# Expert tiles move out of the third and fourth attention round of a one-core decoder layer

## The chip, the core and the metric

The kernel runs on one core of one Trainium2 chip, in one launch. The metric is the device time of an execution in microseconds. Three executions of the kernel before took 701.37, 704.38 and 706.86 us; the median, 704.38 us, is its time.

## What is computed

4096 tokens (64 sequences of 64) of width 128 go through three blocks, each with a residual and a layer norm. Cut to what matters:

```python
def layer(x, ctx):
    x = layernorm(x + state_space_scan(x))                      # 16 states per channel, sequential in time
    x = layernorm(x + gated_linear_attention(q=x, k=ctx, v=ctx)) # 4 heads, exp-gated, causal over 64 tokens
    return layernorm(x + ffn(x))

def ffn(x):                                   # 8 experts, the top 2 for each token, hidden width 512
    probs = softmax(x @ gate_w)
    weight, index = top_k(probs, 2); weight = weight / weight.sum(-1)
    for i in range(8):
        wi = where(index == i, weight, 0).sum(-1)
        h = silu(x @ w1[i]) * (x @ w3[i])
        out += (h @ w2[i]) * wi
    return out
```

## The kernel before

Five instruction lists are written out by hand, one per engine (PE, ACT, DVE, POOL, and SP, which only issues transfers), and tied by semaphores. Each list runs in order. So a list's order is the schedule: an instruction that waits holds back all that stands behind it on its engine.

The tokens are eight chunks of 512 (`NCH = 8`). The first part, up to about 284 us, is the scan, eight steps for each chunk. Then come the attention rounds, c = 0 to 8. Round c on DVE (`attend_round`) normalizes the attention output of chunk c, makes the weights of chunk c + 1 from the scores, and routes chunk c - 1: logits, the two best experts, ranks by PE, and the places of each token's row in a buffer in DRAM sorted by expert. POOL sends these rows there with eight indirect transfers (`send_rows`, L736) at the head of the next round. PE's list for a round has four groups of scores (L979), the transposes of chunk c - 1 (L1008), its logits (L1018), two groups of products with the values (L997), and the rank products (L1028 to L1035).

The experts' work is cut into tiles. The first 25 (`WIDE`) are double tiles of 256 rows of one expert; 21 single tiles of 128 rows are left for the end. A double tile is two units. A unit is two products with `w1` (L1063 into `py` or `pB`), two with `w3`, a Silu on ACT (L1361), and a product on DVE (L1789). The first unit of a tile also carries the product with `w2` of the tile before it (L1076, `down`), scaled on ACT and scattered by POOL (L745). Each tile needs its rows (`load_x`, six buffers) and 768 KB of weights (`load_w`, four buffers). Weights of tile i wait for `down` of tile i - 4.

Which expert and which rows a tile holds is found on the chip. `wide_table`, at the end of a DVE round, turns the counts so far into places for the next tiles, in 17 small operations that each wait for the one before, and three that update the account; `tab_done` is raised. `batch_of(i)` tells which table tile i belongs to. `load_x` waits for this table and for POOL to have sent the rows of all chunks that the table counts.

Where the tiles stand is told by `first_tiles(c)`, spread over the first half of round c's lists, and `second_tiles(c)`, over the second half. Before, these were tile 0 in round 3, tiles 1 and 2 in round 4, and four tiles in each of the rounds 5 to 8; the tiles from 19 on (`LAST_TILES`) lie behind the rounds, six double ones and the 21 single ones. SP loads the second tiles of a round at the head of its round, ahead of the keys (`load_heads`, L493), maxima (`load_m`, L485) and values (`load_v`, L501) of the rounds to come, and the first tiles of the next round behind them. The first input transpose of tiles 0 and 1 (`FRESH`) is placed by hand in rounds 3 and 4; that of any other tile comes with the unit before it. ACT switches its function table between Silu and the logarithm and exponential within a round (`log_exp_table`).

## Time and profile before

| what | us |
|---|---|
| median of three executions | 704.38 |
| the profiled execution | 706.54 |
| its span, first to last instruction | 704.9 |
| TensorE busy | 544.6 (77%) |
| VectorE busy | 430.6 (61%) |
| ScalarE busy | 329.5 (47%) |
| GpSimd (POOL) busy | 369.7 (52%) |
| mean granted TensorE clock | 0.863 of full |

The profile page gives the busy time of each engine, the span in 40 slices, the chain of work that ended last and the costliest groups of instructions. Busy shares are means over stages with different limits, so a change within the attention rounds is read from the rounds: from the timeline of an engine, where each row is a group of instructions with its start, its length, and in brackets how long the engine was idle before it and what ended that, and from windows, one row for each stretch of time: its length, the busy us of PE, PE's weight loads, DVE, ACT and POOL (with their instructions), the granted clock of PE, the DMA engines' busy share and GB/s. The windows shown below are rounds 1, 3, 4, 5, 6 and 7.

### The profile page before, as it was taken

What the parts mean: (1) busy time and instruction counts of PE and PEld (TensorE: products, weight loads), DVE (VectorE), ACT (ScalarE), POOL (GpSimd) and SP (SyncE); (2) the same over time, 40 slices, a digit from 0 to 9 for tenths busy, and PEclk for the clock granted to TensorE, in tenths of its full rate; (3) what the DMA queues carried; (4) which work ended last, traced back from release to release, by engine and by line L of the source; (5) the groups of instructions that cost most, each with busy time, mean ns of one, the idle gap of its engine ahead of it and who ended that gap; (6) DMA issues with size and microseconds to landing.
All of it is one profiled execution on the core that took longest, in us unless ns stands there. A gap on an engine that the chain in (4) does not pass through costs nothing.

```text
span 704.9 us, 10813 instructions
## 1 busy us (share of the span) xinstructions
PE 544.6 (77%) x3387; PEld 386.7 (55%) x3387; DVE 430.6 (61%) x880; ACT 329.5 (47%) x732; POOL 369.7 (52%) x301
## 2 busy tenths in 40 slices
PE   2589999899889888686384889797878689989800
PEld 0234434445344447675263768686667568988800
DVE  1599999999999941676748376656352612211155
ACT  2475685876867553122132435444443323333327
POOL 1497979999789752216506163625253533322341
PEclk9999999999999995555555789998898899999955
DMA  4434535444454532732341735361616157788594
GB/s 148 148 101 148 175 122 166 146 170 167 137 179 146 191 74 52 133 62 62 77 113 42 193 120 158 136 232 36 203 63 216 59 177 243 241 292 270 170 244 117
DMA packets 83319, 104.51 MB, mean 148 GB/s; under 512 B 40784, under 2 KB 64592, under 8 KB 83136
## 3 DMA queue, kind: packets, MB, share of 16 engines
q1 hardware_dynamic: 74576, 90.99, 42.4%
q0 software_dynamic: 4320, 8.92, 3.7%
q10 hardware_dynamic: 4368, 3.93, 2.0%
q8 instruction: 27, 0.44, 0.3%
q14 instruction: 28, 0.23, 0.1%
HBM read 91.48 MB, written 12.34 MB: 147 GB/s over the span
## 4 chain that ended last, share of the span: by engine, by line
PE 25%; issue 24%; POOL 20%; DVE 10%; DMA 9%; ACT 3%; SPq 2%; another core or an unknown queue 1%; POOLq 0%; ACTq 0%; DVEq 0%
POOL hc L640 12%; PE pB L1063 7%; PE pq L1076 4%; DMA wslot<-in_expert_w 4%; PE py L818 4%; PE py L1063 2%; POOL y_dram L745 2%; PE pC L997 1%; ACT x_all L1457 1%; DMA y_dram<-dx,xin 1%; PE pa L979 1%; POOL xg_dram L736 1%; DMA x_all<-y_dram 1%; POOL bcs L604 1%
## 5 line engine op out<-in xcount | busy, mean ns | idle before, releaser
L640 POOL TENSOR_TENSOR hc<-h,Crep 128x1024 f32<-128x1024 f32 x64 | 149.7, 2356 | 14.6 <-DVE h L1507 13.2
L745 POOL DMA_INDIRECT y_dram<-dx,xin x71 | 68.9, 971 | 153.9 <-ACT dx L1378 144.8
L1063 PE MATMUL pB<-Crep,wslot 128*128 128x256 f32 (+1 forms) x556 | 118.9, 360 | 21.9 <-DMA wslot<-in_expert_w 10.7
L818 PE MATMUL py<-hc,ident 128*128 128x512 f32 x256 | 120.7, 598 | 8.1 <-POOL hc L640 8.1
L1063 PEld LDWEIGHTS pB<-Crep,wslot 128*128 128x128 f32 x556 | 90.8, 204 | 38.7 <-DMA wslot<-in_expert_w 14.0
L1498 DVE TENSOR_TENSOR u<-dx,pC 128x1024 f32<-128x1024 f32 x64 | 77.3, 1207 | 17.4 <-PE pC L807 17.3
L818 PEld LDWEIGHTS py<-hc,ident 128*128 128x128 f32 x256 | 46.8, 189 | 53.9 <-issue 37.4
L1789 DVE TENSOR_TENSOR Crep<-u,pB 128x512 f32<-128x512 f32 x35 | 24.0, 686 | 85.5 <-PE pB L1063 42.2
L1507 DVE TENSOR_TENSOR_SCAN h<-pB,u 128x1024 f32<-128x1024 f32 x32 | 73.1, 2285 | 1.0 <-ACT pB L1196 0.6
L1507 DVE TENSOR_TENSOR_SCAN h<-pa,u 128x1024 f32<-128x1024 f32 x32 | 73.1, 2284 | 0.0
L1789 DVE TENSOR_TENSOR u<-u,pB 128x512 f32<-128x512 f32 x36 | 24.8, 688 | 78.9 <-PE pB L1063 46.0
L736 POOL DMA_INDIRECT xg_dram<-x2r,idx x32 | 33.4, 1043 | 41.1 <-DVE idx L1733 32.6
L1378 ACT ACTIVATE dx<-pq,xin 128x128 f32<-128x128 f32 x71 | 23.4, 366 | 66.5 <-PE pq L1076 62.5
L807 PE MATMUL pC<-bcs,sel 96*128 96x512 bf16 x128 | 39.0, 386 | 15.6 <-DVE u L1498 10.0
L1196 ACT ACTIVATE pa<-delta,Aneg 128x512 f32<-128x512 f32 x64 | 41.5, 681 | 20.2 <-DVE h L1507 18.5
L1196 ACT ACTIVATE pB<-delta,Aneg 128x512 f32<-128x512 f32 x64 | 41.5, 679 | 12.4 <-DVE h L1507 12.4
L979 PE MATMUL pa<-x1T_all,dx 32*64 32x64 f32 x512 | 31.7, 289 | 19.6 <-DVE h L1587 8.9
L1063 PE MATMUL py<-Crep,wslot 128*128 128x256 f32 (+1 forms) x180 | 42.3, 370 | 2.6 <-DMA wslot<-in_expert_w 2.5
L1361 ACT ACTIVATE u<-pB 128x512 f32<-128x512 f32 x36 | 21.5, 598 | 47.0 <-PE pB L1063 27.8
L736 POOL DMA_INDIRECT xg_dram<-x2r_last,idx_last x32 | 32.2, 1006 | 19.1 <-DVE idx_last L1733 10.6
L979 PEld LDWEIGHTS pa<-x1T_all,dx 32*64 32x64 f32 x512 | 26.3, 192 | 26.2 <-issue 17.8
L1076 PE MATMUL pq<-wslot,u 128*128 128x128 f32 x288 | 37.8, 283 | 1.3 <-issue 1.3
(225 smaller groups left out, 952.0 us busy)
## 6 DMA issues: line engine op xcount, KB each, us to landing
wslot<-in_expert_w SPq DMA_DIRECT2D x46, 768.0 KB
Crep<-c_dram SPq DMA_DIRECT2D x64, 512.0 KB, 3.8
h<-m_dram SPq DMA_DIRECT2D x16, 256.0 KB
xin<-xg_dram SPq DMA_DIRECT2D x25, 130.0 KB
cT_st<-in_ctx_T SPq DMA_DIRECT2D x8, 256.0 KB, 4.1
dx<-in_ctx_T SPq DMA_DIRECT2D x8, 256.0 KB, 4.0
delta<-in_ctx_tok SPq DMA_DIRECT2D x32, 64.0 KB
hc<-y_dram SPq DMA_DIRECT2D x8, 256.0 KB, 8.5
```

Of the source, the lines that this page charges most:

```text
L640: nc.gpsimd.tensor_tensor(hc[:, K % 4], h[:, K % 3], Crep[:, K % 4].rearrange("p a t -> p (a t)"), ALU.mult).then_inc(hc_done, 1)
L736: nc.gpsimd.indirect_dma_start(out=xg_dram, out_offset=bass.IndirectOffsetOnAxis(ap=places[:, m:m + 1], axis=0), in_=rows[:, k, b], in_off ...
L745: nc.gpsimd.indirect_dma_start(out=y2_dram, out_offset=bass.IndirectOffsetOnAxis(ap=xin[:, i % NX, a, D:D + 1].bitcast(i32), axis=0), in_= ...
L807: last = nc.tensor.matmul(pC[:, i], sel[:, 2 * k + i], bcs[:, c % 2], start=True, stop=True)
L818: last = nc.tensor.matmul(py[:], ident[:], hc[:, K % 4, i * CH:(i + 1) * CH], start=False, stop=(K % STEPS == STEPS - 1 and i == 1))
L979: last = nc.tensor.matmul(pa[S * j:S * j + S, 0, s0:s0 + S], cTc[rows, t0:t0 + S], x1T_all[rows, c * CH + t0:c * CH + t0 + S], start=True, ...
L1063: last = nc.tensor.matmul(bank[:, o * a * P:(o + 1) * a * P], wslot[:, i % NW, stage * F + f * P:stage * F + (f + 1) * P], xgT[i % 2][:, 0 ...
L1076: last = nc.tensor.matmul(pq[:, PAIR + t * P:PAIR + (t + 1) * P], hs[i % 2][:, at:at + P], wslot[:, i % NW, 2 * F + f * D:2 * F + (f + 1) ...
L1196: last = nc.scalar.activation(bank[:, i], delta[:, c % 2], ACT.Exp, scale=Aneg[:, n:n + 1])
L1498: nc.vector.tensor_tensor(u[:, K % 3].rearrange("p (a t) -> p a t", a=2), dx[:, c % 2].unsqueeze(1).to_broadcast([P, 2, CH]), pC[:], ALU.m ...
L1507: nc.vector.tensor_tensor_scan(h[:, K % 3], bank[:].rearrange("p a t -> p (a t)"), u[:, K % 3], 0.0, ALU.mult, ALU.add).then_inc(h_done, 1)
L1789: nc.vector.tensor_tensor(hs[i % 2][:, k * F:(k + 1) * F], sil[:, n % 2], pB[:, 1], ALU.mult).then_inc(mul_done, 1)
```

## The change

Tile 0 no longer stands in round 3 nor tiles 1 and 2 in round 4. Round 5 has five tiles: 0 and 1 in its first half, 2 to 4 in its second. Rounds 6 to 8 have four each (5 to 16), and the tiles from 17 on lie behind the rounds, eight double ones. The first table is made at the end of round 3 in place of round 2 and holds five tiles in place of one, so there is one table less and each tile's number of tables to wait for is one less. SP loads tiles 0 and 1 at the end of its round 3. Only tile 0's transpose is placed by hand, in round 4. ACT's table switches leave rounds 3 and 4.

```diff
--- before.py
+++ after.py
@@ -385,7 +385,7 @@
 
             if i >= WIDE:
                 return NCH
-            return 2 + (i - 1) // TB if i else 1
+            return 2 + max(i - 1, 0) // TB
 
         def first_unit(i):
 
@@ -401,13 +401,15 @@
 
         def first_tiles(c):
 
-            return range(TB * (c - 5) + 3, TB * (c - 5) + 5) if c >= 5 else range(0)
+            if c == 5:
+                return range(0, 2)
+            return range(TB * (c - 5) + 1, TB * (c - 5) + 3) if c >= 6 else range(0)
 
         def second_tiles(c):
 
-            if c == 3:
-                return range(0, 1)
-            return range(TB * (c - 4) + 1, TB * (c - 4) + 3) if c >= 4 else range(0)
+            if c == 5:
+                return range(2, TB + 1)
+            return range(TB * (c - 5) + 3, TB * (c - 4) + 1) if c >= 6 else range(0)
 
         def units(tiles):
 
@@ -504,7 +506,7 @@
             def load_x(i):
                 b = batch_of(i)
                 a = halves(i)
-                sp.wait_ge(tab_done, b)
+                sp.wait_ge(tab_done, b - 1)
                 top_row = E * REG + (SPARE - 1) * P if a == 1 else E * REG - PAIR
                 row = sp.value_load(rowt[0:1, i:i + 1], min_val=0, max_val=top_row)
                 sent = min(b, NCH - 1)
@@ -549,7 +551,9 @@
                 if c == 2:
                     store_m(1)
                     load_m(c + 3)
-                if 4 <= c < NCH:
+                if c == 3:
+                    load_tiles(first_tiles(5))
+                if 5 <= c < NCH:
                     load_tiles(first_tiles(c + 1))
             before, behind = range(LAST_TILES.start, WIDE - 2), range(WIDE - 2, WIDE)
             load_tiles(before)
@@ -1078,7 +1082,7 @@
                                                 start=(f == 0), stop=(f == FB - 1))
                 last.then_inc(dn_done, 1)
 
-            FRESH = (0, 1)
+            FRESH = (0,)
 
             def expert_units(numbers):
                 for n in numbers:
@@ -1127,8 +1131,8 @@
                 if front:
                     scores(c + 1, 3)
                     weighted_values(c + 1, 0)
-                if c in (3, 4):
-                    turn_x(c - 3)
+                if c == 4:
+                    turn_x(0)
                 expert_units(second[0:1])
                 if front:
                     weighted_values(c + 1, 1)
@@ -1379,7 +1383,7 @@
                                                 scale=xin[:, i % NX, a, D + 1:D + 2])
                 last.then_inc(y_cp, 1)
 
-            FRESH = (0, 1)
+            FRESH = (0,)
 
             def expert_units(numbers):
                 for n in numbers:
@@ -1419,7 +1423,7 @@
                 if mid:
                     square_heads(c)
                 expert_units(first[1:2])
-                if mid and c >= 4:
+                if mid and c >= 5:
                     log_exp_table()
                 if front:
                     weight_decay(c + 1)
@@ -1430,10 +1434,10 @@
                     copy_rows(c - 1)
                 if c == 3:
                     floor_gates(1)
-                if c in (3, 4):
-                    copy_xT(c - 3)
+                if c == 4:
+                    copy_xT(0)
                 expert_units(second[0:2])
-                if c >= 3:
+                if c >= 5:
                     log_exp_table()
                 if back:
                     share_exp(c - 1)
@@ -1771,11 +1775,11 @@
 
             def wide_table(c):
 
-                n = 1 if c == 1 else TB
-                if c == 1:
+                n = TB + 1 if c == 2 else TB
+                if c == 2:
                     dve.wait_ge(const_step, CONSTS)
                 dve.wait_ge(ranks_read, c + 1)
-                table(region, ALU.is_ge, PAIR, TB * (c - 2) + 1 if c > 1 else 0, n)
+                table(region, ALU.is_ge, PAIR, TB * (c - 2) + 1 if c > 2 else 0, n)
                 tlink(nc.vector.tensor_scalar(cum[:], cum[:], float(PAIR * n), None, ALU.min))
                 tlink(nc.vector.tensor_tensor(given[:, 0:E], given[:, 0:E], cum[:], ALU.add))
                 tlink(nc.vector.tensor_tensor(given[:, 1:E], given[:, 1:E], cum[:, 0:E - 1], ALU.subtract))
@@ -1855,7 +1859,7 @@
                 if c == 3:
                     log_norm(1)
                 attend_round(c)
-                if c >= 2:
+                if c >= 3:
                     wide_table(c - 1)
                 if c == 0:
                     keep_gates(NCH - 1)
```

Three places of the lists, before and after. The lines of the changed kernel are two to four higher.

VectorE at the end of round 2, before. `idx_last` are the places of chunk 1's rows; what follows is the table, up to the running maximum `mrow` and the next round's first operation `norm`.

```order
L1733 CAST idx_last<-posf 128x8
L1750 TENSOR_TENSOR cnt<-carry,region 128x8
L1751 TENSOR_TENSOR ysq<-cnt,kstep 128x8x16
L1753 TENSOR_REDUCE ntl<-ysq 128x8
...
L1766 CAST eoff<-tsum 128x1
L1768 CAST rowt<-tsum 128x1
L1779 TENSOR_SCALAR cum<-cum 128x8
L1780 TENSOR_TENSOR given<-given,cum 128x8
L1781 TENSOR_TENSOR given<-given,cum 128x7
L1537 SCALAR_TENSOR_TENSOR mrow<-fence,pq 128x128
L1542 TENSOR_TENSOR nlog<-cs_sb,pq 128x48
L1596 TENSOR_TENSOR norm<-pC,floor_ 128x16
```

The same place now:

```order
L1737 CAST idx_last<-posf 128x8
L1541 SCALAR_TENSOR_TENSOR mrow<-fence,pq 128x128
L1546 TENSOR_TENSOR nlog<-cs_sb,pq 128x48
L1600 TENSOR_TENSOR norm<-pC,floor_ 128x16
L1579 TENSOR_TENSOR u<-u,g_sb 128x1024
```

The table is gone from this place; the first one stands at the end of round 3.

TensorE in the second half of round 3, before: `pa` are scores, `pC<-delta,h` the products with the values, `xin` the tile's rows, `wslot` its weights, `mask` the ranks.

```order
L979 MATMUL pa<-x1T_all,dx 64x64 x16
L997 MATMUL pC<-delta,h 64x33 x16
L1046 MATMUL pq<-ident,xin 128x128 x2
L1063 MATMUL pB<-Crep,wslot 128x256 x4
L997 MATMUL pC<-delta,h 64x33 x16
L1063 MATMUL py<-Crep,wslot 128x256 x2
L1063 MATMUL pB<-Crep,wslot 128x256 x2
L1028 MATMUL pC<-mask,tri_s 128x32
```

The same stretch now:

```order
L983 MATMUL pa<-x1T_all,dx 64x64 x16
L1001 MATMUL pC<-delta,h 64x33 x32
L1032 MATMUL pC<-mask,tri_s 128x32
```

The tile's transpose and its eight products have left round 3. In round 4 only tile 0's transpose stands between the two groups of products with the values.

VectorE at the end of round 5, before (`u<-u,pB` or `Crep<-u,pB` is a unit's product, `pos` the first operation on the ranks):

```order
L1712 TENSOR_TENSOR x2r<-share 128x4
L1789 TENSOR_TENSOR u<-u,pB 128x512
L1650 TENSOR_SCALAR xT<-plog,mv,rstd 128x128 x4
L1789 TENSOR_TENSOR u<-u,pB 128x512
L1718 TENSOR_TENSOR pos<-pC,carry 128x32
L1722 TENSOR_TENSOR carry<-carry,pC 128x8
```

The same place now:

```order
L1716 TENSOR_TENSOR x2r<-share 128x4
L1793 TENSOR_TENSOR Crep<-u,pB 128x512
L1654 TENSOR_SCALAR xT<-plog,mv,rstd 128x128 x4
L1793 TENSOR_TENSOR Crep<-u,pB 128x512
L1793 TENSOR_TENSOR u<-u,pB 128x512 x2
L1722 TENSOR_TENSOR pos<-pC,carry 128x32
L1726 TENSOR_TENSOR carry<-carry,pC 128x8
```

Two more unit products, those of the fifth tile, stand ahead of the ranks.

## Rows read from the trace of the kernel before

**Rows 1.** Windows by round: length, busy PE, PEld, DVE, ACT, POOL, PEclk, DMA.

```profile
303.00:319.30 16.30, 11.75 (x150) 10.36 (x149) 15.03 (x57) 4.33 (x10) 2.35 (x1) 0.50 0.34 62
...
343.90:376.50 32.60, 22.04 (x202) 17.37 (x200) 17.97 (x76) 9.30 (x17) 10.00 (x9) 0.55 0.40 93
376.50:412.50 36.00, 26.98 (x242) 23.06 (x242) 21.29 (x77) 15.13 (x28) 14.88 (x14) 0.74 0.56 155
412.50:449.40 36.90, 33.05 (x284) 28.21 (x284) 23.71 (x80) 17.92 (x34) 18.51 (x18) 0.91 0.46 144
449.40:486.10 36.70, 30.35 (x252) 25.59 (x252) 21.87 (x81) 17.84 (x34) 16.18 (x17) 0.95 0.39 130
486.10:522.50 36.40, 30.84 (x167) 26.14 (x168) 19.17 (x73) 16.89 (x33) 15.34 (x17) 0.86 0.38 129
```

**Rows 2.** Timeline of VectorE: where rounds 1, 3, 4 and 5 begin and end.

```profile
303.04 0.17 DVE L1596 TENSOR_TENSOR norm<-pC,floor_ 128x16 f32<-128x16 f32 x1
...
319.02 0.17 DVE L1733 CAST idx<-posf 128x8 int32<-128x8 f32 x1
...
338.61 0.17 DVE L1733 CAST idx_last<-posf 128x8 int32<-128x8 f32 x1
...
342.75 0.42 DVE L1537 TENSOR_TENSOR_SCAN mrow<-fence,pq 128x128 f32<-128x128 f32 x1
...
343.86 0.17 DVE L1596 TENSOR_TENSOR norm<-pC,floor_ 128x16 f32<-128x16 f32 x1
...
376.45 0.17 DVE L1596 TENSOR_TENSOR norm<-pC,floor_ 128x16 f32<-128x16 f32 x1
...
408.19 0.17 DVE L1733 CAST idx_last<-posf 128x8 int32<-128x8 f32 x1
...
412.49 0.17 DVE L1596 TENSOR_TENSOR norm<-pC,floor_ 128x16 f32<-128x16 f32 x1
```

**Rows 3.** Timeline of VectorE in the tail: first unit products of two tiles.

```profile
575.87 0.69 DVE L1789 TENSOR_TENSOR Crep<-u,pB 128x512 f32<-128x512 f32 x1 [3.83 <-PE pB L1063]
...
587.54 0.69 DVE L1789 TENSOR_TENSOR Crep<-u,pB 128x512 f32<-128x512 f32 x1 [1.28 <-PE pB L1063]
```

**Rows 4.** Timelines of POOL and SP in round 4: first send, loads of tile and keys.

```profile
373.12 0.98 POOL L736 DMA_INDIRECT xg_dram<-x2r,idx  x1 [20.46 <-DVE idx L1733]
...
385.44 0.40 SPq L517 DMA_DIRECT2D xin<-xg_dram  x1
...
389.35 0.43 SPq L493 DMA_DIRECT2D dx<-in_ctx_T  x1
```

**Rows 5.** Timeline of PE: waits for rows and weights, rounds 4, 6 to 8, tail.

```profile
391.17 3.78 PE L1063 MATMUL pB<-Crep,wslot 128*128 128x256 f32 x8 [1.91 <-DMA wslot<-in_expert_w]
...
466.61 1.99 PE L1063 MATMUL pB<-Crep,wslot 128*128 128x256 f32 x8 [0.59 <-DMA wslot<-in_expert_w]
...
499.42 0.44 PE L1046 MATMUL pq<-ident,xin 128*128 128x128 f32 x2 [0.91 <-DMA xin<-xg_dram]
...
503.11 2.65 PE L1063 MATMUL pB<-Crep,wslot 128*128 128x256 f32 x8 [2.39 <-DMA wslot<-in_expert_w]
...
539.22 1.99 PE L1063 MATMUL pB<-Crep,wslot 128*128 128x256 f32 x8 [2.00 <-DMA wslot<-in_expert_w]
...
573.78 1.99 PE L1063 MATMUL pB<-Crep,wslot 128*128 128x256 f32 x8 [2.52 <-DMA wslot<-in_expert_w]
```

**Rows 6.** Timeline of PE: the last two groups of scores, rounds 1 and 3.

```profile
309.64 2.29 PE L979 MATMUL pa<-x1T_all,dx 32*64 32x64 f32 x32 [2.00 <-DVE h L1587]
...
352.86 2.29 PE L979 MATMUL pa<-x1T_all,dx 32*64 32x64 f32 x32 [3.61 <-DVE h L1587]
```

**Rows 7.** Timeline of VectorE in round 3: the copy of the logits.

```profile
351.17 0.19 DVE L1667 COPY lgc<-pC 128x32 f32<-128x32 f32 x1 [3.26 <-remote]
```

**Rows 8.** Timeline of PE in round 5: the same four products, early and later.

```profile
416.88 2.05 PE L1063 MATMUL py<-Crep,wslot 128*128 128x256 f32 x4
...
425.83 1.13 PE L1063 MATMUL py<-Crep,wslot 128*128 128x256 f32 x4
```

## What the change is predicted to do

> **What bounds the kernel now.** I read the granted clock and span first, then the page's slices, then the busy times of each attention round (the windows [rows 1]), then the timeline of VectorE (DVE), whose in-order list marks where each round begins [rows 2], then PE, SP and POOL inside the rounds, and last the steady part of the tail. A round begins on DVE with `norm<-pC,floor_` (L1596). So round 1 begins at 303.04, round 3 at 343.86, round 4 at 376.45, round 5 at 412.49. The reader is to see two kinds of round. Round 1 has no expert tile and takes 16.3 us. Rounds 5 and 6 carry four double tiles each in 36.9 and 36.7 us, with PE busy for 33.05 and 30.35 us at a granted clock of 0.91 and 0.95 [rows 1]: they are near PE's bound. Rounds 3 and 4 carry one and two double tiles, yet take 32.6 and 36.0 us at a clock of 0.55 and 0.74 [rows 1]. So the first three tiles are the dearest of all: over a bare round with a table (16.3 + 4.3 us, the table's size is worked out below) they cost 68.6 - 41.2 = 27.4 us together, 9.1 each, where a double tile behind the rounds takes 5.84 us (rows of products 11.67 us apart over two tiles [rows 3]). The reason stands in the same rows: their matmuls run at the half clock, their two banks of products are waited for in DVE's order ahead of routing work, and in round 4 the tile's own rows and weights arrive late, because SP can load them only once POOL has sent the routed rows: POOL's first send is at 373.12, SP's load at 385.44, and PE's first product waits for the weights until 391.17 [rows 4, 5].
>
> **The change part by part.** All sums are made against the profiled execution: 706.54 us, of which the span is 704.9 and 1.6 lies around it. It is 2.2 us (0.3%) above the median of 704.38; I carry the difference over to the median.
>
> Round 2 loses its table (17 small DVE operations and three that update the account). idx_last is written at 338.61 and the next operation that stays, `mrow`, stands at 342.75 [rows 2]: 4.14 us. In order without the table the next operation follows in about 0.1 us. DVE is alone on the path here, since PE's transpose and round 3 both wait for `mrow`. So -4.0 us. The table of round 3 now makes five places in place of four; its instructions are the same number and one column longer, nothing to count.
>
> Round 3 without its tile: from its start to the two last score products is 352.86 - 343.86 = 9.0 us, which stays as it is [rows 2, 6]. From there a bare round goes on as round 1 does: 309.64 to the places at 319.02 is 9.4 us. Then the table, from places to the next round: 408.19 to 412.49, 4.3 us [rows 2, 6]. That is 22.7 us against 376.45 - 343.86 = 32.6. So -9.9 us. Those 9.0 us hold a wait of 3.26 us that the trace puts to "remote" [rows 7], at DVE's copy of the logits; I leave it in. If it goes, 3.3 us more are saved.
>
> Round 4 without its two tiles: 319.02 - 303.04 = 16.0 us for a bare round up to the places, and 4.3 for the table: 20.3 us against 412.49 - 376.45 = 36.0 [rows 2]. So -15.7 us. Up to here 29.6 us are saved, and round 5 begins near 383.
>
> Round 5 gets a fifth double tile. Its two units stand behind one another at the end of the round (the piece of order shows four products in a row, where two stood). Nothing of DVE's is between them, and DVE's ranks, places and table wait behind them. So they cost the steady rate of the tail: +5.8 us [rows 3]. Lower bound: nothing, if they fill idle time of PE, but PE is idle for only 3.9 of 36.9 us there. Upper bound: what a tile costs in round 4, (36.0 - 20.3)/2 = 7.9 us. I take 5.8.
>
> What the start of round 5 meets is new. The tiles 0 and 1 are loaded by SP behind round 3's loads, and must wait for POOL's sends: from the first send to the load it was 385.44 - 373.12 = 12.3 us [rows 4]. The places of round 3 come at about 358.2, so the sends begin at about 359.1 and the load goes out at about 371.4. Queued behind it on SP are tile 0's weights, tile 1, and then the keys of round 5's scores (`dx`), 3.9 us later (385.44 to 389.35 [rows 4]), at about 375.3. PE would ask for them at the end of round 4, some 14 us after its start at 362.5, so at about 376.5; with two weight tiles ahead of them on the same engines they may land at 380 or 381. PE then stands for up to 4 us, while DVE still has until 382.8 + 2.5 us of its own work. PE also turns tile 0 in round 4, between the two products with the values: it waits perhaps 1 us for the rows. I take +1.5 us, bounds 0 and 5.
>
> Round 5 starts at the half clock, as before: the same four products took 2.05 us at 416.88 and 1.13 us at 425.83 [rows 8]. The idle 3.9 us of PE lie at the start of the round, where the logits wait for DVE, then and now. What is new is that the two rounds in front are cold too. I add nothing for it in the sum and keep it as a rival.
>
> Rounds 6 to 8 and the tail keep their number of tiles per round, but every tile is now one to two tiles older when used: round 6 takes 5 to 8 where it took 7 to 10. Before, the third tile of each of these rounds is of the newest batch. It waits for POOL's sends through SP, and PE stands for the weights: 0.59 us in round 6, 0.91 and 2.39 in round 7, 2.00 in round 8, 2.52 in the tail [rows 5]. In the changed order the third tile of round 6 is of a batch whose table was made in round 4. Its load waits for nothing but a free place among four. So the 5.9 us of rounds 6 to 8 should go. Bounds: 0 (another wait takes their place) and 9 (round 7 also runs part of its time at the half clock, mean 0.86 [rows 1]). I take -5.
>
> The tail has eight double tiles in place of six: two at 5.84 = +11.7 us [rows 3]. But the newest tile (21) is now fifth in the tail where it was third, so the wait of 2.5 us goes too: +9.2 us. The 21 single tiles and all behind them are untouched.
>
> Sum: -4.0 - 9.9 - 15.7 + 5.8 + 1.5 - 5.0 + 9.2 = -18.1 us. On the profiled execution that is 688.4; on the median 686.3. What hid some of this was never idle DVE time: rounds 3 and 4 were long because their tiles stood inside DVE's list, so moving them out shortens the rounds at once, and what is late next is the bare round's own chain (DVE 15.03 us busy of 16.3 in round 1 [rows 1]).
>
> **Rivals.** A: less is gained. The waits of the late weights are replaced and not removed (+5), the 3.3 us stall of round 3 comes once more in round 4 as PE and DVE go through their lists faster (+3), and round 5's keys cost the whole 5 (+3.5 over mine) with part of these together: about 9 us, so 695. For it: stalls put to no visible cause stand in the bare stretches (3.26 us [rows 7]). Against it: round 1 has none.
>
> B: more is gained. The stall of round 3 goes (-3.3), the late loads give the full 9 (-4), the keys are hidden (-1.5): 8.8 more, about 677.5. For it: round 7 has no scores to make and still takes 36.4 us [rows 1], so its waits and its slow clock do set its length.
>
> C: slower. The clock. In rounds 3 and 4 PE now has only some 12 us of work in each 20, as in round 1 with its clock at 0.50 [rows 1]. If the gate stays at half through the whole of round 5, its products take 2.05/1.13 = 1.8 times as long. PE's work there is 33 us, of which about 3 are the price of the slow start, plus 5.8: 36 us at the full clock, 65 at half. With the 3.9 idle that is 69 us where I have 44, and 2 more at the start of round 6: +27, so about 713. It decides from where the half clock lasts over two thirds of round 5. Against it: in round 5 the clock was back within 9 us, between the products at 416.88 and 425.83 [rows 8], out of a round that began after an idle stretch as well. The Trainium skill (TensorE: Matmul & The Clock Gate, What's actually happening) says that the default state is throttled and activity releases it. By that rule the dense start of round 5 gives the clock back, and the row agrees; the two idle rounds ahead of it would cost nothing more.
>
> D: no change: round 5's five tiles and the tail's two take what they took where they were (9.1 us each): 27.4 us given back of 29.6, so about 702. Against it: the price of those three was the half clock, the late rows and the tables around them, none of which moves along.
>
> **How the numbers follow.** My case 0.66, with its own range 680 to 694; A 0.15; B 0.12; D 0.04; C 0.03. The predicted time is 686.3. The range reaches over A and most of B: 676 to 698. A measurement of this kernel can tell about 1% (7 us) from no change. Faster by over 1% means under 697.3: my case, B and most of A, 0.91. Within 1%: the rest of A and D, 0.06. Slower: C, 0.03.
>
> **What would show it.** In the changed profile: round 3 near 23 us and round 4 near 20 with no L1067 product in them; no DVE work between `idx_last` and `mrow` in round 2; round 5 at 43 to 46 us, with the half clock over before its second tile is through; no DMA wait of PE over 1 us in rounds 6 to 8 nor at the tail's fifth tile; round 7 at 33 us or less; 12 us more between the tail's first product and its first single tile, less 2.5. I am wrong if round 4 stays above 25 us, if round 5 goes over 50, or if PE's waits for weights come back in rounds 6 to 8.

## The result, and the profile after

The changed kernel takes 673.14 us (median of four, 670.91 to 674.23) where the kernel before took 702.91 beside it: a ratio of 0.9564 [0.9514, 0.9615]. I had forecast 686.3, with a range of 676 to 698. The direction was right; the gain is 29.8 us where I had 18.1, and the time falls below the range. Between the two profiled executions, spans 704.9 and 669.3, it is 35.6 us: the changed kernel's profiled execution was its fastest, and that of the kernel before, at 706.54 us, lies 3.6 above this median.

The changed kernel was measured in five batches of runs, and in two of them (one of these a single execution) it took 684 us, with stalls in its trace that the section on the hardware describes; I compare runs of one batch, or name it. The changed kernel was not run beside newest_wait, tile0_round3 and tiles01_round4; their traces show none of the stalls, so they are set against 673.14.

The windows of the changed kernel, one row a stage, with the columns of [rows 1]: rounds 2 to 8 (the last ends at the places), the table behind it, the eight double tiles of the tail, its single tiles.

```profile
319.30:337.80 18.50, 11.06 (x138) 9.76 (x140) 16.01 (x58) 4.32 (x10) 11.67 (x10) 0.50 0.25 61
337.80:360.00 22.20, 14.17 (x184) 12.38 (x182) 19.55 (x73) 5.13 (x12) 13.33 (x12) 0.50 0.56 103
360.00:381.30 21.30, 10.34 (x133) 9.28 (x133) 19.28 (x73) 4.11 (x10) 11.03 (x10) 0.50 0.53 146
381.30:421.90 40.60, 39.38 (x345) 33.17 (x344) 25.84 (x83) 22.13 (x42) 19.27 (x18) 0.97 0.65 189
421.90:458.30 36.40, 31.51 (x252) 27.07 (x252) 21.79 (x80) 17.90 (x34) 16.19 (x16) 0.91 0.41 130
458.30:490.00 31.70, 29.38 (x170) 24.73 (x170) 19.64 (x77) 16.76 (x33) 15.91 (x17) 0.89 0.47 151
490.00:511.10 21.10, 20.59 (x124) 16.72 (x122) 9.00 (x34) 11.45 (x23) 12.58 (x14) 1.00 0.60 205
511.10:520.00 8.90, 3.38 (x24) 2.75 (x22) 7.47 (x35) 1.55 (x5) 6.12 (x7) 0.82 0.49 158
520.00:567.50 47.50, 46.73 (x260) 38.50 (x261) 11.00 (x16) 15.24 (x37) 16.96 (x18) 0.93 0.53 169
567.50:630.20 62.70, 60.47 (x509) 58.34 (x508) 13.76 (x20) 22.64 (x60) 20.11 (x21) 1.00 0.80 269
```

Read it against [rows 1]: rounds 3 and 4 are bare (22.2 and 21.3 us for 32.6 and 36.0), round 5 is now the densest round (PE busy 39.4 of 40.6 us, clock 0.97), round 7 lost 5 us, and round 8 is all PE: 20.59 of 21.10 us at the full clock. That last row is the one I had not foreseen. The marks of DVE's list, which answer [rows 2]:

```profile
336.60 0.17 DVE L1737 CAST idx_last<-posf 128x8 int32<-128x8 f32 x1
336.68 0.41 DVE L1541 TENSOR_TENSOR_SCAN mrow<-fence,pq 128x128 f32<-128x128 f32 x1
337.78 0.17 DVE L1600 TENSOR_TENSOR norm<-pC,floor_ 128x16 f32<-128x16 f32 x1
...
360.01 0.17 DVE L1600 TENSOR_TENSOR norm<-pC,floor_ 128x16 f32<-128x16 f32 x1
...
381.25 0.17 DVE L1600 TENSOR_TENSOR norm<-pC,floor_ 128x16 f32<-128x16 f32 x1
```

`mrow` follows `idx_last` at once: the table has left round 2. The stages one by one, in us, from such marks; "second trace" is another execution of the kernel before (the first experiment).

| stage | forecast | before | second trace | after |
|---|---|---|---|---|
| round 2 | -4.0 | 24.5 | 22.6 | 18.5 |
| round 3 | -9.9 | 32.6 | 29.8 | 22.2 |
| round 4 | -15.7 | 36.0 | 36.2 | 21.2 |
| round 5 | +7.3 | 36.9 | 36.9 | 40.6 |
| round 6 | | 36.7 | 36.6 | 36.5 |
| round 7 | | 37.0 | 35.4 | 31.7 |
| round 8 to the places | -5.0 for 6 to 8 | 29.6 | 31.8 | 21.1 |
| places to the tail's first product | 0 | 9.0 | 8.9 | 8.9 |
| double tiles of the tail | +9.2 | 37.5 | 40.3 | 47.5 |
| single tiles | 0 | 66.4 | 66.2 | 62.7 |

### The profile page after: what moved, and what is told of

It is laid out like the page before. It is cut to its first block, busy times and chain, and to the rows that moved or that the text cites. A ratio compares the mean times of both kernels' runs of the same rounds, so it can differ in the third digit from the quotient of the medians.

```text
span 669.3 us, 10788 instructions
## 1 busy us (share of the span) xinstructions
PE 534.1 (80%) x3387; PEld 378.9 (57%) x3387; DVE 433.3 (65%) x862; ACT 321.8 (48%) x727; POOL 371.1 (55%) x301
## 4 chain that ended last, share of the span: by engine, by line
PE 32%; POOL 21%; issue 15%; DVE 13%; DMA 7%; ACT 4%; SPq 1%; POOLq 0%; ACTq 0%; DVEq 0%
POOL hc L644 13%; PE pB L1067 10%; PE pq L1080 5%; PE py L822 4%; PE py L1067 3%; POOL y_dram L749 2%; PE pa L983 2%; DMA dx<-in_ctx_T 2%; ACT x_all L1461 1%; PE pC L1001 1%; DMA y_dram<-dx,xin 1%; DMA x_all<-y_dram 1%; PE pq L1050 1%; POOL xg_dram L740 1%; DMA Crep<-c_dram 1%
## 5 line engine op out<-in xcount | busy, mean ns | idle before, releaser
L822 PE MATMUL py<-hc,ident 128*128 128x512 f32 x256 | 122.2, 605 | 7.9 <-POOL hc L644 7.9
L1067 PE MATMUL pB<-Crep,wslot 128*128 128x256 f32 (+1 forms) x556 | 113.4, 348 | 7.7 <-DVE Crep L1793 6.8
L1067 PEld LDWEIGHTS pB<-Crep,wslot 128*128 128x128 f32 x556 | 87.2, 198 | 23.3 <-DVE Crep L1793 10.4
L811 PE MATMUL pC<-bcs,sel 96*128 96x512 bf16 x128 | 39.0, 386 | 15.7 <-DVE u L1502 10.2
L1200 ACT ACTIVATE pa<-delta,Aneg 128x512 f32<-128x512 f32 x64 | 41.4, 678 | 20.3 <-DVE h L1511 18.4
L740 POOL DMA_INDIRECT xg_dram<-x2r_last,idx_last x32 | 32.6, 1019 | 23.6 <-DVE idx_last L1737 15.0
L1067 PE MATMUL py<-Crep,wslot 128*128 128x256 f32 (+1 forms) x180 | 39.4, 352 | 1.0 <-DMA wslot<-in_expert_w 1.0
L729 POOL TENSOR_TENSOR u<-maskT,h 128x1024 f32<-128x1024 f32 x8 | 18.8, 2352 | 35.6 <-ACT h L1329 20.6
```

What stands on the lines that cost most here:

```text
L740: nc.gpsimd.indirect_dma_start(out=xg_dram, out_offset=bass.IndirectOffsetOnAxis(ap=places[:, m:m + 1], axis=0), in_=rows[:, k, b], in_off ...
L811: last = nc.tensor.matmul(pC[:, i], sel[:, 2 * k + i], bcs[:, c % 2], start=True, stop=True)
L822: last = nc.tensor.matmul(py[:], ident[:], hc[:, K % 4, i * CH:(i + 1) * CH], start=False, stop=(K % STEPS == STEPS - 1 and i == 1))
L1067: last = nc.tensor.matmul(bank[:, o * a * P:(o + 1) * a * P], wslot[:, i % NW, stage * F + f * P:stage * F + (f + 1) * P], xgT[i % 2][:, 0 ...
L1200: last = nc.scalar.activation(bank[:, i], delta[:, c % 2], ACT.Exp, scale=Aneg[:, n:n + 1])
```

## Experiments

All are the changed kernel with one edit, unless said. The ratio is to the kernel before, run in the same batch.

**The kernel before, once more** (no edit; 704.65 us, one execution).

> The kernel before, once more, for a second trace. Theory 1 (the stalls that the first trace of it puts to no cause, 4.5 us in round 2, 3.3 us in round 3 and 4.7 us of DVE at the start of round 8, belong to the instruction lists): they stand again in the same places, within 1 us. Theory 2 (they belong to that one execution): at least two of the three are gone and the time is 3 to 6 us under the first profile's 706.5.

The stalls of rounds 2 and 3 that had no cause in the first trace are gone (22.6 and 29.8 us), but the time is only 1.9 us below the 706.54 of the first profile. In round 8 a wait stands plainly that the first trace had covered up. PE's timeline there:

```profile
529.23 0.69 PE L1046 MATMUL pq<-ident,xin 128*128 128x128 f32 x2 [6.34 <-DMA xin<-xg_dram]
...
532.38 3.78 PE L1063 MATMUL pB<-Crep,wslot 128*128 128x256 f32 x8 [0.76 <-DMA wslot<-in_expert_w]
```

PE waits 6.34 us for the rows of the newest tile, then 0.76 for its weights, and the eight products behind it run at the half clock, 3.78 us in place of 1.99 [rows 5]. In the first trace the same place showed a wait of 2.00 us. So what the older tiles take away in round 8 is about 10 us and not 2. A third trace (before_ref2) has the same rounds 2 and 3 and the same wait, 6.35 us for the rows.

**The wait put back** (newest_wait). SP waits for the sends of the newest places before it loads the second half of the tiles of rounds 6 to 8, so that the third tile of each of these rounds waits for what it waited for in the kernel before:

```diff
             for c in range(-1, NCH + 1):
+                if c >= 6:
+                    sp.wait_ge(rows_sent[c % 2], 128 * ((c - 2) // 2 + 1))
                 load_tiles(second_tiles(c))
```

> The changed kernel, in which SP, before it loads the second tiles of rounds 6, 7 and 8, waits until POOL has sent the rows of that round's newest chunk, as the kernel before had to. Theory 1 (the late weights are what shortened rounds 7 and 8 by 5.3 and 7 us): PE waits 0.5 to 3 us for weights again in each, its clock falls there, and the time rises by 6 to 12 us, to 679 to 685. Rival (those rounds were long by stalls of other kinds): PE's waits come back but the time rises by under 3 us.

Measured: 695.17 us, ratio 0.9879 [0.9834, 0.9924]. PE's timeline of round 7, then of round 8:

```profile
483.06 0.44 PE L1052 MATMUL pq<-ident,xin 128*128 128x128 f32 x2 [2.88 <-DMA xin<-xg_dram]
486.82 3.78 PE L1069 MATMUL pB<-Crep,wslot 128*128 128x256 f32 x8 [2.46 <-DMA wslot<-in_expert_w]
...
521.26 0.69 PE L1052 MATMUL pq<-ident,xin 128*128 128x128 f32 x2 [7.07 <-DMA xin<-xg_dram]
524.65 3.78 PE L1069 MATMUL pB<-Crep,wslot 128*128 128x256 f32 x8 [1.00 <-DMA wslot<-in_expert_w]
```

Rounds 6, 7 and 8 grow by 5.3, 8.0 and 11.8 us (to 41.8, 39.7 and 32.9); round 5 is 4.8 longer, by its clock alone, which the edit does not touch. The same two waits and the same half clock behind them are back. This settles the largest step: the wait for the newest rows in rounds 6 to 8 is worth 15 to 25 us, with the clock that it costs, far more than the 6 to 12 expected. It overshoots what the change took away (14). PE waits longer for the third tile here than in the first trace before: 2.50 us for 0.59 in round 6, and 5.34 for 3.30 in round 7.

**The wait in round 8 alone** (wait_round8): the same line under `if c == 8`.

> The changed kernel, in which SP waits, before the second tiles of round 8 alone, for the rows of that round's newest chunk. Theory (the wait for the newest rows in round 8, which the second trace of before shows as 6.3 us for rows and 0.8 for weights with a fall of the clock behind it, is the largest single part of what I missed): round 8 goes from 21 to over 30 us and the time rises by 9 to 12 us, to 682 to 685. Rival (the waits of rounds 6 and 7 and an early start of the tail make most of it): it rises by under 4 us.

Measured: 690.63 us, 0.9768 [0.9684, 0.9851], beside 683.93 for the changed kernel in the same batch (one execution). Round 8 takes 33.3 us against 26.6: +6.7. The median moves by 6.7 too, though the execution whose rounds these are is 9.3 over. That is less than the 9 to 12 expected, and more than the rival's 4. In this batch round 8 was already 5 us longer by stalls, which may cover part of the wait.

**Tile 0 back in round 3, its table in round 2** (tile0_round3).

```diff
             if c == 5:
-                return range(2, TB + 1)
+                return range(3, TB + 1)
...
+            if c == 3:
+                return range(0, 1)
...
-                if c >= 3:
+                if c >= 2:
                     wide_table(c - 1)
```

> The changed kernel with tile 0 back in round 3 and its one-place table back in round 2; round 5 then holds tiles 1 to 4, everything else stays. Theory of the recorded sum: +4.0 for the table, +10 for round 3, -5.8 for the tile that leaves round 5: +8, near 681. Rival (a tile in round 5 costs less than 4 us, since it fills PE's idle time and keeps the clock up): +10 to +12, near 684. If tiles cost the same wherever they stand: +4, near 677.

Measured: 677.39 us, 0.9653 [0.9612, 0.9693]. Round 2 is 22.6 (+4.1), round 3 is 30.3 (+8.1), round 5 with four tiles 35.3 (5.3 to 8.4 less than round 5 of the changed kernel, by its trace). So the part that frees rounds 2 and 3 is worth 12.2 us there and costs 5 to 8 in round 5: 4 to 7 net, where the medians say 4.3. The sum of the prediction would have it at 8 (681 us); the measured time is the one expected if a tile cost the same wherever it stands.

**Tiles 0 and 1 back in round 4** (tiles01_round4).

```diff
+            if c == 4:
+                return range(0, 2)
             if c == 5:
-                return range(2, TB + 1)
+                return range(4, TB + 1)
```

> The changed kernel with tiles 0 and 1 used in round 4 (as two tiles were before) and 2 to 4 in round 5, everything else stays. Theory of the recorded sum: +15 for round 4, -11.7 for two tiles less in round 5: +3, near 676. Rival (tiles in round 5 cost under 4 us each): +7 to +9, near 681. If tiles cost the same wherever they stand: no change.

Measured: 682.49 us, 0.9709 [0.9674, 0.9744]. Round 4 takes 38.1 us at a clock of 0.67; round 5 has only three tiles and still takes 38.0, at 0.78. Two tiles in a cold round cost 16.9 us, and taking two away from round 5 gave back 3 to 6, by the traces of the changed kernel without stalls: the sparser round did not keep its clock. The sum of the prediction had 11.7 there and 676 us in all; the expected rival, tiles in round 5 at under 4 us each and near 681, is what came.

**Four tiles in round 5, nine behind the rounds** (nine_behind).

```diff
-            return range(TB * (c - 5) + 1, TB * (c - 5) + 3) if c >= 6 else range(0)
+            return range(TB * (c - 5), TB * (c - 5) + 2) if c >= 6 else range(0)
...
-                return range(2, TB + 1)
-            return range(TB * (c - 5) + 3, TB * (c - 4) + 1) if c >= 6
+                return range(2, TB)
+            return range(TB * (c - 5) + 2, TB * (c - 4)) if c >= 6
```

> The changed kernel with four tiles in round 5 and nine double tiles behind the rounds: one tile goes from the round to the tail. Theory of the recorded sum (5.8 us in either place): round 5 down by 5.8, the tail up by 5.8, no change, 673 within 2. Rival (in the round it fills idle time of PE, the fifth tile having cost only 3.7 us): up by 2 to 3 us.

Measured: 689.5 us, 0.9753 [0.9665, 0.984], in the batch where the changed kernel had 683.93. Round 5 gives back 7.0 (37.5), the tail's double tiles take 5.6 more (52.9), and round 6, with the same four tiles, takes 5.7 more (41.6): its clock is 0.84, where it is 0.90 in the changed kernel of that batch, and a stall of PE of 1.88 us stands in it, which no releaser explains. Whether the clock is lower because round 5 has less to do, this run doesn't show. The 7.0 and 5.6 are near the steady 5.8 in either place, as the sum of the prediction had it, though executions of one list differ by 5 us in round 5. The 5.6 us by which the whole is longer stand in round 6, partly in a stall, so that the tile is better placed in round 5 than behind the rounds is not shown.

**The keys of round 5 ahead of the tiles on SP** (keys_first). PE waits at the end of round 4:

```profile
379.77 1.11 PE L983 MATMUL pa<-x1T_all,dx 32*64 32x64 f32 x16 [4.56 <-DMA dx<-in_ctx_T]
```

I had asked whether this wait is part of the path.

```diff
                 load_tiles(second_tiles(c))
-                if c + 2 < NCH:
+                if c == 4:
+                    load_heads(6)
+                    load_tiles(first_tiles(5))
+                if c + 2 < NCH and c != 4:
                     load_heads(c + 2)
...
-                if c == 3:
-                    load_tiles(first_tiles(5))
```

> The changed kernel in which SP loads the keys of round 5's scores ahead of tiles 0 and 1. The trace of after has PE waiting 4.56 us for them at the end of round 4. Theory 1 (the recorded term: that wait costs about 1.5 us): the wait goes and the time falls by 1 to 2 us. Theory 2 (PE's work there was ahead of DVE anyway, and with the keys early PE is idle later, at the logits of round 5, as in all other rounds, and starts at the half clock): the wait goes, an idle 3 to 4 us appears at the logits, and the time stays within 1 us or rises by up to 3.

Measured: 684.2 us, 0.9686 [0.9607, 0.9765]: as the changed kernel in that batch. The wait for `dx` is gone, and PE waits for DVE at the logits of round 5:

```profile
388.65 1.03 PE L1023 MATMUL pC<-rw,Crep 128*128 128x8 f32 x8 [1.61 <-DVE Crep L1615]
```

That is 1.6 us, less than half of the 3 to 4 expected. The rest of the gain went into the clock: it is full from 388 to 390, then 0.56 and 0.58 in the next two stretches of 2 us, where it is 1.00 in the changed kernel's trace. Round 4 takes 21.2 us with the late keys and with the early ones: up to the end of that round they were hidden by DVE's list.

**The tail's wait for DVE** (tail_spread). In the changed kernel PE waits once in the tail, for DVE's last tables:

```profile
520.77 5.49 PE L1067 MATMUL pB<-Crep,wslot 128*128 128x256 f32 x12 [6.28 <-DVE Crep L1793]
```

The edit puts the first of the tail's unit products ahead of those tables, and one more behind every five of their steps:

```diff
                 dve.wait_ge(t_step, steps[0])
+                if spread[0]:
+                    links[0] += 1
+                    if links[0] % 5 == 0:
+                        product_h(next(tail))
```

> The changed kernel with the two tables behind round 8 cut into pieces of five operations, with the tail's first unit ahead of them and one unit's product between the pieces. In the traces PE is idle for 6.3 us behind round 8 and then runs some 5 us at the half clock. If DVE's table is what it waits for: 6 to 10 us less than after_ref. Rival (the rows of the newest tile are late instead): under 3 us less.

Measured: 684.38 us, 0.9703 [0.9653, 0.9753], beside 684.68 in the same batch: nothing. The tail begins 8.3 us earlier (524.6 for 532.9), and then PE waits for something else:

```profile
540.03 0.66 PE L1050 MATMUL pq<-ident,xin 128*128 128x128 f32 x2 [6.96 <-ACT dx L1382]
```

The trace puts ACT's own wait there, 9.37 us, to "remote". By the lists its scaling of the outputs has no free buffer, since the scatters that empty the buffers stand between and behind POOL's eight sends of routed rows, four and four. The next run tests that.

**The same, with POOL's sends in pairs between the scatters** (tail_pool_spread).

```diff
-            send_rows(NCH - 1, 0)
-            scatters(LAST_TILES[0:1])
-            send_rows(NCH - 1, 1)
-            scatters(LAST_TILES[1:])
+            send_rows(NCH - 1, 0, (0, 1))
+            scatters(LAST_TILES[0:1])
+            send_rows(NCH - 1, 0, (2, 3))
+            scatters(LAST_TILES[1:2])
+            send_rows(NCH - 1, 1, (0, 1))
+            scatters(LAST_TILES[2:3])
+            send_rows(NCH - 1, 1, (2, 3))
+            scatters(LAST_TILES[3:])
```

> The changed kernel with the tables behind round 8 cut into pieces as in tail_spread, and with POOL's eight sends of the last rows given out in pairs between the scatters of four tiles. In tail_spread PE's idle 6.3 us for DVE came back as 7.0 us for ACT's scaling, which waits for a free output buffer, thus for scatters that stand behind four sends. If POOL's order is all that gave it back: the tail's first 8 double tiles close up and the time falls by 5 to 9 us against after_ref3. Rival (the last table or the newest tile's rows become late by the spreading): under 2 us.

Measured: 673.13 us, 0.9554 [0.9504, 0.9604], beside 673.59 in the same batch: nothing again. ACT's long wait is gone, as it should be if POOL's order was its cause, and PE's wait has moved a third time, to the rows and weights of the newest tile, whose sends now end later:

```profile
536.64 0.69 PE L1054 MATMUL pq<-ident,xin 128*128 128x128 f32 x2 [3.08 <-DMA xin<-xg_dram]
540.03 3.78 PE L1071 MATMUL pB<-Crep,wslot 128*128 128x256 f32 x8 [1.00 <-DMA wslot<-in_expert_w]
```

**The tables behind the next round's first product** (table_later), and that with tail_spread (both_tables).

```diff
                 expert_units(first[0:1])
+                if c >= 4:
+                    wide_table(c - 2)
                 mid(5, 6)
...
-                if c >= 3:
+                if c == NCH:
                     wide_table(c - 1)
```

> The changed kernel with each table of rounds 3 to 7 moved behind the next round's first unit product, so that the attention output is normalized 4.3 us earlier and PE's logits don't wait 3.7 us. Theory (PE is the bound of rounds 6 to 8 and each idle stretch there also costs a start at the half clock): 3.7 us and 2 to 4 us of clock in rounds 6 and 7 each: 8 to 15 us less than after_ref. Rival (the rounds' length is set by DVE's chain, of which the table stays a part): under 4 us less.

> Both edits together. If they act on separate stretches, the sum of the two: 14 to 25 us less than after_ref; if one takes what the other needs, no more than the better of them.

Measured: 689.06 us, 0.9765 [0.9703, 0.9827], and 690.47, 0.9792 [0.9711, 0.9872]; the changed kernel had 684.68. No gain came, where 8 to 15 and 14 to 25 us were expected. Each round hands its table to the next, so round 3 is one table shorter (18.6 for 22.9) and round 8 one longer (30.8 for 26.4), and rounds 5 and 6 lose 2.3 and 2.1 besides. The wait at the logits of rounds 6 and 7 is gone, and in its place the second unit waits. PE's timeline in rounds 5 to 7:

```profile
395.36 3.75 PE L1067 MATMUL pB<-Crep,wslot 128*128 128x256 f32 x8 [4.17 <-issue]
...
440.01 3.86 PE L1067 MATMUL pB<-Crep,wslot 128*128 128x256 f32 x8 [6.15 <-issue]
...
475.39 3.26 PE L1067 MATMUL pB<-Crep,wslot 128*128 128x256 f32 x8 [4.19 <-issue]
```

The last operations of the table stand at 392.24, 434.56 and 472.27 in DVE's timeline, so PE waits on for 3 to 5 us behind them. This batch has the stalls, and at the place of the first of these waits the changed kernel has one of 3.32 us itself (below). How much belongs to the table and how much to the stalls isn't separated.

**The changed kernel again, in four batches** (after_again, after_ref, after_ref2, after_ref3), and the kernel before again (before_ref2). No edits.

> The changed kernel once more, for a second trace. If where the clock returns in round 5 (at 383.5 us in the first trace, 4 us after PE began; at 392.5 in the run with the old wait, whose list is the same up to there) is chance, it falls somewhere in 383 to 393 and round 5 takes 40.5 to 45.5 us; if it belongs to the list, round 5 takes 40.6 again. Rounds 3, 4 and 8 repeat within 0.5 us either way.

> The changed kernel, timed on this chip with the three below. If the gain belongs to the change alone: 671 to 675. If part of the gain hangs on the chip or on where PE's clock and its causeless stalls fall (the second trace had 5 us more in round 8, 4 us more in round 5, 2 us more in round 2 than the first): up to 685.

> The changed kernel on one more chip. Theory 1 (two levels, each belonging to a chip or to where a load of the program lies): all its executions are near 672 (rounds 2 and 8 at 18.5 and 21 us, none of PE's causeless stalls) or all near 684 (20.4 and 26.5 us, with them). Rival (chance of each execution): a mix.

> The kernel before on the same chip, for its trace. If the same stalls strike it, round 2 takes 24.5 us (22.6 without), but round 8 loses little by them, since PE waits there for the newest tile's rows anyway (6.3 us in the second trace of before): 701 to 706 on either level.

> The changed kernel as the reference of the run below: 668 to 674 on a chip on which PE has no causeless stalls, 683 to 686 on one with them.

Measured: 683.93 (one execution); 684.68, 0.9708 [0.9659, 0.9757]; 670.82, 0.9532 [0.9484, 0.9581]; 673.59, 0.9552 [0.9473, 0.9631]. The kernel before: 699.25 in one execution, and 702 to 705 as the median of every batch. So the changed kernel has two levels, 671 to 674 and 684, and the kernel before has one. PE's timeline of rounds 2 and 3 at the upper level (after_ref), then the same places at the lower one, on the same chip (after_ref3):

```profile
327.89 1.12 PE L983 MATMUL pa<-x1T_all,dx 32*64 32x64 f32 x16 [1.34 <-PE pa L983]
...
350.58 1.12 PE L983 MATMUL pa<-x1T_all,dx 32*64 32x64 f32 x16 [2.98 <-remote]
...
392.74 3.75 PE L1067 MATMUL pB<-Crep,wslot 128*128 128x256 f32 x8 [3.32 <-issue]
```

```profile
328.16 2.29 PE L983 MATMUL pa<-x1T_all,dx 32*64 32x64 f32 x32 [1.89 <-DVE h L1591]
...
346.67 2.29 PE L983 MATMUL pa<-x1T_all,dx 32*64 32x64 f32 x32 [1.81 <-DVE h L1591]
```

At the upper level PE stops in the middle of the 32 scores, for 1.34 and 2.98 us, between two instructions that wait for nothing that explains it; at the lower level the 32 run through. Round 2 takes 20.4 and 18.5 us, round 8 26.4 and 21.1.

**PE's list moved by 64 and by 128 instructions** (pe_shift64, pe_shift128), to see whether the stalls hang on where an instruction lies in PE's program.

```diff
+            for _ in range(64):
+                pe.sem_inc(passed, 1)
             pe.wait_ge(step_weights, 80)
```

> The changed kernel with 64 semaphore increments at the head of PE's list, in its first wait, which move all that follows to later places in PE's instruction stream. Theory A (PE's causeless stalls come from fetching its own instructions at fixed distances of the stream): on a chip of the slow level the stalls move to other instructions or vanish, and rounds 2 and 8 change by over 1 us each. Theory B (they come from elsewhere: the transfers of POOL, the chip): they stay at the same places and the time stays within 1.5 us of after_ref2. On a chip of the fast level neither shows.

> The same with 128 increments: as above, with other places again by theory A, and no change by theory B.

Measured: 671.8 us, 0.9571 [0.952, 0.9621], and 681.65, 0.972 [0.9653, 0.9787], beside 670.82. Every round of both is as in the changed kernel; the 10 us of the second are a late start (PE's first matmul stands at 20.41 us, where it stood at 9.61). But this batch was at the lower level throughout, so there was no stall to move, and only PE's list was shifted, not ACT's or DVE's. The question stays open.

## Why the prediction was right, and where it was wrong

**Round 2, -4.0: right.** 22.6 to 18.5 us against the second trace. The 6.0 against the first hold 1.9 us of a stall.

**Rounds 3 and 4, -9.9 and -15.7: right**, at 22.2 and 21.2 us for a forecast of 22.7 and 20.3. Two errors cancel in round 3. The "remote" wait of 3.26 us [rows 7], which I had left in, went (the scores stand 6.6 us behind the round's start, as in round 1, and not 9.0). And from there to the places it is 11.3 us and not round 1's 9.4: an operation of DVE's beside a product of POOL's is stretched by 2.8 us where it was 1.65 in round 1 (shown below), and DVE waits 0.63 us for PE's scores. The same stretch adds 1.0 in round 4.

**Round 5, +7.3: too much in this trace.** It grew by 3.7. But the same list takes 40.6 to 45.6 us over its executions, which is 3.7 to 8.7 more than before, stalls included, and has the 7.3 inside. The steady cost of the fifth tile is borne out roughly by nine_behind, which gives 7.0 back for it. What was wrong is that the keys' wait, sized right (4.56 us, forecast "up to 4"), costs nothing: keys_first took it away and gained nothing, since a gap at the logits and the half clock behind it came in its place. With the keys late PE begins the round without that gap, and in this trace the clock was full some 4 us after that dense start (the 16 scores at 384.48 take 0.68 us, where they take 1.11 at 379.77). The Trainium skill (TensorE: Matmul & The Clock Gate, What's actually happening) says that activity releases the throttle; the rows agree, though not on a fixed time (last section). Rival C, that the two cold rounds in front would hold the clock down, is refuted by the 0.97 of round 5.

**Rounds 6 to 8, -5: this is the step that failed.** The mechanism was the right one (tiles one batch older no longer wait for POOL's sends through SP), but the term was mis-sized: it is -14.0 against the first trace and -14.5 against the second. Of the 14.0, 5.3 are in round 7 and 8.5 in round 8. I added up the waits of PE that one trace put to a DMA [rows 5]: 0.59, 0.91 and 2.39, 2.00. Three things were missing from that sum. In round 8 the 2.00 us stood in a trace where stalls (4.55 us of DVE put to "issue" and 4.71 to "remote") had already used up the time; without them the same wait is 6.34 and 0.76. In a round where PE has nothing but tiles, a wait also costs the clock: products of 1.99 us take 3.78 behind it. And the windows that I had shown end at round 7 [rows 1]. Round 8 of the first trace, in the same columns:

```profile
522.50:552.20 29.70, 23.90 (x124) 19.29 (x123) 9.06 (x35) 11.23 (x23) 13.16 (x14) 0.89 0.46 156
```

PE is the only engine near its limit there, and it is idle for 5.8 us and has its clock at 0.89 besides. The same 124 instructions take 20.59 us in the changed kernel. That row would have shown 5.8 us, and with the clock 8.4 (23.90 busy us at 0.89 in place of 1.00 are 2.6 more). The upper bound that I gave (9) came from round 7's clock and took nothing of round 8 but its 2.00. newest_wait shows that the wait is the cause: put back, it costs 25 us over the three rounds.

**Tail, +9.2: right.** 10.0 against the first trace, 7.2 against the second, 9.9 against the third. The wait of 2.5 us at the newest tile went, as said.

**Single tiles, 0.** They are 3.7 us shorter, and whether that is the change isn't shown: this stretch took 66.4, 66.2 and 63.4 us in three traces of the kernel before, and between 61.4 and 64.9 in five of the changed one, with the same work in it. It is a part of why the profiled executions differ by more than the medians, together with the stalls.

**The rivals.** B (more is gained, 677.5) was the nearest. Of its three parts the stall of round 3 went and the late loads gave their all and 5 more; the keys were hidden. Its chance of 0.12 was too low, and the sign of my own case (no transfer that PE waits for in rounds 6 to 8) held. A and D are refuted by the table; C by the clock. In two of the five batches the changed kernel takes 684, next to my 686. But that is chance, since those stalls were no term of my sum.

None of these edits beats the changed kernel.

## What to carry to other kernels

A wait that the trace puts to a transfer is worth what the stage would be without it, not its own length: set each stage's length against its busy time at the full clock, for every stage, also the one in which the main work has run out, since there a wait costs its length and the clock behind it. Take a second trace of the same kernel before sizing a wait of a few us: a stall without a cause in front of it can hide most of it. And an idle gap is worth moving work into only if what stands behind it is not waiting for a third engine: the tail's 6 us moved from DVE to POOL to the newest rows, and the time never changed.

## What the runs showed of the hardware that I had not expected

**DVE is held up beside a product of POOL's.** In rounds 1 to 4 of the changed kernel one operation of DVE in each is stretched to the end of a product of POOL's, or just past it. Three of them in DVE's timeline, then POOL's:

```profile
309.34 1.84 DVE L1679 TENSOR_TENSOR tie<-lgc,top 128x32 f32<-128x32 f32 x1
...
347.56 3.53 DVE L1633 TENSOR_TENSOR Crep<-Crep,onorm 128x512 f32<-128x512 f32 x1
...
367.04 2.81 DVE L1687 TENSOR_TENSOR hot<-tie,tmax 128x32 f32<-128x32 f32 x1
```

```profile
308.78 2.35 POOL L729 TENSOR_TENSOR u<-maskT,h 128x1024 f32<-128x1024 f32 x1 [14.84 <-ACT h L1329]
...
348.17 2.36 POOL L729 TENSOR_TENSOR u<-maskT,h 128x1024 f32<-128x1024 f32 x1
...
367.43 2.36 POOL L729 TENSOR_TENSOR u<-maskT,h 128x1024 f32<-128x1024 f32 x1
```

`tie` ends at 311.18 and POOL's product at 311.13; `hot` at 369.85 and 369.79. `Crep` ends at 351.09, 0.56 behind it. The operations take 0.19 us elsewhere, and `Crep` 0.69. So DVE loses 1.65 us in round 1 and 2.3 to 2.8 in rounds 2 to 4, where DVE is the path, and my yardstick, round 1, had less of it inside. The Trainium skill (SBUF — State Buffer, SBUF: two separate sides) says that the two engines share a port pair that one holds for a whole instruction; the common ends agree with it, though `Crep` and `hot` are recorded as beginning 0.6 and 0.4 us ahead of POOL's product. No run here moved the product away, so the cause rests on these coincidences.

**Two levels of one kernel.** In two of six batches PE stalls for 1 to 5 us in rounds 2, 3, 5 and 8 in every trace of the changed kernel, mostly with no releaser. Round 8 loses the most, 5.3 to 5.5 us, and there the stall isn't PE's alone: in after_ref PE waits 3.41 us for ACT's scaling, which itself stood for 3.79 us, put to "remote". The chip is not the cause: chip 1 showed both levels in two batches. It is no property of a single execution either: the four of after_ref lie within 1.6 us. The first trace of the kernel before had such stalls (round 2 at 24.5 us), the trace of the changed kernel that I set against it had none. What differs between batches is not in the trace, and the cause stays open. That the kernel before has one level would fit if it spent the same stalls within its waits: its round 8 takes 29.6 us in the trace with stalls and 31.8 without. No run tests this, and its executions differ by up to 8 us within a batch.

**The clock's return varies.** With one and the same list, round 5 takes 40.6, 41.2, 41.4, 43.7, 44.5 and 45.6 us; the last two are at the upper level and hold stalls of 1.5 and 3.3 us. Round 5 of newest_wait has the same list and no such stall, and takes 45.4. There the four products at 388.01 still take 2.05 us, and those at 396.82 take 1.13:

```profile
388.01 2.05 PE L1069 MATMUL py<-Crep,wslot 128*128 128x256 f32 x4
...
396.82 1.13 PE L1069 MATMUL py<-Crep,wslot 128*128 128x256 f32 x4
```

In the changed kernel's trace the same four stand at 386.00 and take 1.11. Both begin their dense work at 379.7. In the changed kernel's trace the granted clock is 0.50 up to 382 and 1.00 from 384. In newest_wait PE is busy all the time from 380 on, and the clock is 0.50 in every stretch of 2 us up to 392 and 1.00 only from 394. So the clock came back about 4 us after the dense start in one execution and about 13 us after it in another, which makes some 5 us between the two. What decides it, no run shows.
